# A recurrent two-tower scorer in fp32: the path's second layers as single products of 512 columns, and all engine orders rewritten with the path one step further ahead

## The reference, cut to what matters

```python
def _tower(x, w_in, b_in, blocks):
    h = _leaky(x @ w_in + b_in)
    for w1, b1, w2, b2 in blocks:          # two blocks, all 128 wide
        h = _leaky(_leaky(h @ w1 + b1) @ w2 + b2 + h)
    return h
...
def step(prev_delta, xk):
    fk, k = xk
    d = jnp.where(k == 0, fk[:, DELTA_IDX], jax.lax.stop_gradient(prev_delta))
    fk = fk.at[:, DELTA_IDX].set(d)
    fe = _tower(fk[:, :N_FLAT], fw_in, fb_in, flat_blocks)
    pe = _tower(fk[:, N_FLAT:], pw_in, pb_in, path_blocks)
    h = _leaky(jnp.concatenate([fe, pe], axis=-1) @ cw1 + cb1)
    delta = jax.nn.sigmoid(h @ cw2 + cb2)[:, 0]
    return (delta, delta)
```

## Time and profile before

| | |
|---|---|
| median of 3 runs | 1264.81 us (1264.74 to 1265.58) |
| the profiled execution's own time | 1264.49 us |
| its span in the trace | 1262.7 us |
| PE busy | 1243.4 us, 98% |
| PEld busy | 1062.1 us, 84% |
| ACT busy | 931.3 us, 74% |
| DVE busy | 888.8 us, 70% |
| POOL busy | 23.0 us, 2% |

### The profile page before, as it was taken

One profiled execution on the slowest core, in us unless ns is written; L12 is line 12 of the kernel. 1 busy time (PEld: TensorE's weight loads), 2 busy tenths in 40 slices (PEclk: granted clock), 3 DMA queues, 4 the chain that ended last, 5 costly groups with the idle time before them and its releaser, 6 DMA issues.

```text
span 1262.7 us, 20315 instructions
## 1 busy us (share of the span) xinstructions
PE 1243.4 (98%) x6022; PEld 1062.1 (84%) x6022; DVE 888.8 (70%) x1933; ACT 931.3 (74%) x2049; POOL 23.0 (2%) x20
## 2 busy tenths in 40 slices
PE   5999999999999999999999999999999999999998
PEld 3788888888888888888888888888888888888886
DVE  3677777777777777777777777777777777767775
ACT  2677777777777777777777777777777777777776
POOL 6000000000000000000000000000000000000000
PEclk9999999999999999999999999999999999999999
DMA  4400000000000000000000000000000000000000
GB/s 156 195 12 10 10 13 10 9 12 10 10 10 12 10 10 12 10 10 11 12 10 10 12 10 10 12 10 10 11 12 10 9 12 11 10 11 12 10 8 2
DMA packets 14177, 23.53 MB, mean 19 GB/s; under 512 B 6468, under 2 KB 6904, under 8 KB 13304
## 3 DMA queue, kind: packets, MB, share of 16 engines
q1 hardware_dynamic: 13640, 22.23, 6.0%
q10 hardware_dynamic: 432, 0.01, 0.0%
HBM read 15.66 MB, written 6.55 MB: 18 GB/s over the span
## 4 chain that ended last, share of the span: by engine, by line
PE 98%; DVE 1%; ACT 0%; issue 0%; DMA 0%; SPq 0%; DVEq 0%; ACTq 0%
PE ps_path L466 35%; PE ps_flat L466 18%; PE ps_res L469 18%; PE ps_head L567 9%; PE ps_head L562 9%; PE ps_path L484 2%; PE ps_head L580 2%; PE ps_head L575 2%; PE ps_flat L530 2%; DVE f_in L371 0%; DMA hidden_w<-hidden 0%; DVE p_sum L374 0%; PE ps_res L466 0%; DVE f_t L407 0%; SPq L201 0%
## 5 line engine op out<-in xcount | busy, mean ns | idle before, releaser
L257 ACT ACTIVATE f_mid<-ps_flat,columns_sb 128x256 f32<-128x256 f32 x512 | 242.7, 474 | 164.7 <-PE ps_flat L466 158.3
L466 PE MATMUL ps_path<-p_mid,hidden_w 128*128 128x256 f32 x1024 | 306.6, 382 | 0.8 <-ACT p_mid L257 0.8
L469 PE MATMUL ps_res<-f_mid,hidden_w 128*128 128x256 f32 x1024 | 305.6, 380 | 0.2
L257 ACT ACTIVATE f_res<-ps_res 128x256 f32<-128x256 f32 x512 | 196.4, 384 | 63.3 <-PE ps_res L469 63.3
L466 PEld LDWEIGHTS ps_path<-p_mid,hidden_w 128*128 128x128 f32 x1024 | 191.4, 191 | 33.2 <-ACT p_mid L257 2.4
L469 PEld LDWEIGHTS ps_res<-f_mid,hidden_w 128*128 128x128 f32 x1024 | 168.7, 189 | 54.1 <-ACT f_mid L257 1.7
L374 DVE SCALAR_TENSOR_TENSOR p_sum<-ps_path,columns_sb,p_in 128x512 f32<-128x512 f32 x128 | 96.1, 751 | 137.1 <-PE ps_path L466 137.1
L257 ACT ACTIVATE p_mid<-ps_path,columns_sb 128x512 f32<-128x512 f32 x256 | 176.2, 688 | 5.3 <-PE ps_path L466 5.3
L435 DVE CAST head_hi<-head 128x256 fp32r<-128x256 f32 x256 | 75.3, 294 | 136.2 <-ACT head L257 136.2
L407 DVE SCALAR_TENSOR_TENSOR f_t<-delta,columns_sb,ps_flat 128x256 f32<-128x256 f32 x256 | 123.2, 481 | 49.6 <-ACT delta L312 49.2
L466 PE MATMUL ps_flat<-f_in,hidden_w 128*128 128x256 f32 x512 | 153.2, 381 | 4.6 <-DVE f_in L371 4.5
(11 more groups left out here) (46 smaller groups left out, 1453.1 us busy)
## 6 DMA issues: line engine op xcount, KB each, us to landing
x_path<-x_hi SPq DMA_DIRECT2D x256, 16.0 KB
x_path<-x_lo SPq DMA_DIRECT2D x256, 16.0 KB
x_flat<-x_hi SPq DMA_DIRECT2D x256, 6.0 KB
x_flat<-x_lo SPq DMA_DIRECT2D x256, 6.0 KB
chunk_x<-x SPq DMA_DIRECT2D x2, 1152.0 KB, 7.2
x_hi<-chunk_hi SPq DMA_DIRECT2D x2, 1152.0 KB, 8.4
x_lo<-chunk_lo SPq DMA_DIRECT2D x2, 1152.0 KB, 10.1
out<-delta SPq DMA_DIRECT2D x128, 2.0 KB
```

The source lines that it names most:

```text
L257: return act.activation(dst, src, ACT.Prelu, bias=bias, alpha=NEG)
L466: return pe.matmul(dst, weight[w_name], src, start=True, stop=True)
L469: return pe.matmul(dst, weight[w_name], src, start=False, stop=True, skip_group_check=True)
```

## The change

LEAD becomes 4. `path_1b` and `path_2b` on PE lose their argument h and become one product of 512 columns each. The bodies of PE, ACT and DVE are written in a new order: the flat chain of group 1 now begins earlier (`flat_1a`, `flat_1b` and `flat_2a` of step k + 1 stand at the end of body k), `path_in` and `path_1a` work on step k + 4, `path_1b` on k + 4 (PE), `path_2a` and `path_2b` on k + 2. SP's and POOL's programs are unchanged. Lines 484 and below move up or down by a few: L530, L562, L567, L575 and L580 are L524, L556, L561, L569 and L574 after the change.

```diff
-LEAD = 3
+LEAD = 4
...
@@ ACT
             def body(k):
                 flat_1a(k, 0)
-                flat_1b(k, 1)
+                flat_2b(k, 1)
                 flat_1b(k, 0)
-                flat_2a(k, 1)
+                path_in(k + 4)
+                head_out(k, 1)
                 flat_2a(k, 0)
-                flat_2b(k, 1)
-                path_1b(k + 2)
+                path_2a(k + 2)
                 flat_2b(k, 0)
-                head_out(k, 1)
+                delta_out(k, 1)
                 head_out(k, 0)
-                path_in(k + 3)
-                delta_out(k, 1)
-                path_2a(k + 2)
+                path_1a(k + 4)
+                flat_1a(k + 1, 1)
                 delta_out(k, 0)
-                path_1a(k + 3)
-                flat_1a(k + 1, 1)
+                flat_1b(k + 1, 1)
+                path_1b(k + 3)
+                flat_2a(k + 1, 1)
...
@@ DVE
             def body(k):
                 flat_delta(k, 0)
                 flat_in(k, 0)
-                flat_1b_old(k, 1)
+                flat_2b_old(k, 1)
                 flat_1b_old(k, 0)
-                path_1b_sum(k + 2)
-                flat_2b_old(k, 1)
+                path_1b_sum(k + 3)
+                path_2b(k + 1)
                 flat_2b_old(k, 0)
-                path_2b_sum(k + 1)
-                path_2b(k + 1)
                 head_high(k, 1)
                 head_low(k, 1)
+                flat_delta(k + 1, 1)
+                flat_in(k + 1, 1)
                 head_high(k, 0)
                 head_low(k, 0)
-                flat_delta(k + 1, 1)
-                flat_in(k + 1, 1)
+                flat_1b_old(k + 1, 1)
+                path_2b_sum(k + 2)
...
@@ PE
-            def path_1b(k, h):
-                if exists(k):
-                    if h == 0:
-                        pe.wait_ge(s_p1a_h, k + 1)
-                        product(half(ps_path1, h), "pr1_w2", half(p_mid1, h))
-                    else:
-                        product(half(ps_path1, h), "pr1_w2", half(p_mid1, h)).then_inc(s_p1b_mm, 1)
+            def path_1b(k):
+                if exists(k):
+                    pe.wait_ge(s_p1a_h, k + 1)
+                    product(ps_path1[:, :], "pr1_w2", p_mid1[:, :]).then_inc(s_p1b_mm, 1)
...
```

More of the change, by code:

```diff
@@ L513, in path_2a, with path_2b @@
                         product(half(ps_path2, h), "pr2_w1", half(p_res1[par], h)).then_inc(s_p2a_mm, 1)
-            def path_2b(k, h):
+            def path_2b(k):
                 if exists(k):
-                    if h == 0:
-                        pe.wait_ge(s_p2a_h, k + 1)
-                        product(half(ps_path2, h), "pr2_w2", half(p_mid2, h))
-                    else:
-                        product(half(ps_path2, h), "pr2_w2", half(p_mid2, h)).then_inc(s_p2b_mm, 1)
+                    pe.wait_ge(s_p2a_h, k + 1)
+                    product(ps_path2[:, :], "pr2_w2", p_mid2[:, :]).then_inc(s_p2b_mm, 1)
             def flat_x(k, g):
@@ L584, in body @@
                 flat_1a(k, 0)
-                flat_1b(k, 1)
-                path_1b(k + 2, 1)
+                combine_path(k, 0)
+                flat_2b(k, 1)
                 flat_1b(k, 0)
-                flat_2a(k, 1)
-                path_2b(k + 1, 1)
+                flat_x(k + 1, 1)
+                path_in(k + 4)
+                combine_flat(k, 1)
                 flat_2a(k, 0)
-                flat_2b(k, 1)
-                combine_path(k, 0)
+                path_2a(k + 2, 0)
+                path_2a(k + 2, 1)
+                output_high(k, 1)
                 flat_2b(k, 0)
-                combine_flat(k, 1)
-                flat_x(k + 1, 0)
-                path_in(k + 3)
-                combine_flat(k, 0)
-                flat_x(k + 1, 1)
-                path_2a(k + 2, 0)
-                output_high(k, 1)
-                path_2a(k + 2, 1)
-                output_low(k, 1)
-                output_high(k, 0)
-                path_1a(k + 3, 0)
-                output_low(k, 0)
-                path_1a(k + 3, 1)
-                combine_path(k + 1, 1)
-                path_2b(k + 2, 0)
-                flat_1a(k + 1, 1)
-                path_1b(k + 3, 0)
+                output_low(k, 1)
+                path_1a(k + 4, 0)
+                path_1a(k + 4, 1)
+                combine_flat(k, 0)
+                path_2b(k + 2)
+                flat_1a(k + 1, 1)
+                output_high(k, 0)
+                combine_path(k + 1, 1)
+                output_low(k, 0)
+                flat_x(k + 1, 0)
+                flat_1b(k + 1, 1)
+                path_1b(k + 4)
+                flat_2a(k + 1, 1)
             pe.wait_ge(s_w_loaded, 16)
```

## The result

The changed kernel takes 1283.67 us (1283.22 to 1284.86, 4 runs) against 1264.78 (1264.64 to 1265.58): a ratio of 1.0147 [1.0135, 1.0159], or 18.9 us more. The forecast was 1276.5 with a range up to 1282.0. The direction was right; the loss was larger than the range allowed.

A forecast was written before the change was run, and what follows sets the result against it. PE was taken to bound the kernel, busy 98% at full clock with 9.58 us a step. The terms -1.2 + 4.6 + 2.3 + 4.6 + 1.7 gave +12.0 on 1264.5, so 1276.5 us, range 1269.5 to 1282.0.

The forecast's parts named there:

- Part 1: Merged path_1b and path_2b products on PE: two passes fewer each save 0.005 us a product, -1.2 us in all.
- Part 2: Group 1's second flat layer on PE: a wait of 0.036 us for ACT's f_mid in every step, +4.6 us.
- Part 3: The fill: path's chain and POOL's hold on DVE's p_res2 delay the first flat product, +2.3 us.
- Part 4: path_in of step 6: PE waits for loads queued behind chunk stores, +4.6 us, then half clock, +1.7 us.
- (c): Rival: a second thin cover also gives way, or the clock falls more often; 10 us more, 1286 us; chance 0.07.

The follow-up runs named there:

- x2_split: The changed kernel with path_1b and path_2b again as two products of 256 columns each, in the merged one's place: 1283.76 us, ratio 1.015.

## Why the prediction was wrong in size

**Part 1 (-1.2): nothing measurable.** The merged product's two passes start 0.429 us apart, 0.858 for a product where I had 0.863; the two products that x2_split has in its place take 0.863. So the 0.005 is there at the product, but the step shows 0.002 of the 0.010, and the runs show none.

**Part 2 (+4.6): the term that was mis-sized most.** With part 1 the forecast had 0.027 us a step; it is 0.061, over 127 steps 7.7 us in place of 3.4. ACT's part, 0.036, was right (0.033 with DVE's order mended). The sentence that failed is that no operation on DVE or ACT stands behind one that is ready later "except at the place named". flat_1b_old(k+1, 1) had all its inputs and stood behind head_low, which waits for ACT's head. I had looked at the durations of the new queue, and for the second layer at its wait for ACT alone, though its other input had moved to a new place. That is 0.028 a step, 3.5 us: DVE's add ends no later than f_mid, but its signal needs 0.12 us to the weight load and f_mid's 0.05. In the new place that is enough to bind PE.

**Long steps (no term): +1.5.** The kernel before has one, and it is the same thing: its head_low at 158.77 is DVE's number 319, 0.37 us late.

```profile
158.77 0.42 DVE L441 TENSOR_TENSOR head_lo<-head,head_hi 128x256 fp32r<-128x256 f32 x1 [0.48 <-DVE head_hi L435]
```

Its number 1983, at 851.09, is 0.32 late and lengthens no step. So the lateness was there before the change, and the covers took most of it. That DVE's places go by its own instructions is shown; what happens there is not, nor where TensorE's places lie and why two of them (36 and 39) moved with DVE's instructions. My rule for how far long steps move fell.

**Part 3 (+2.3): +2.46, the right number by luck.** The first flat product came at 35.87, some 0.2 late, and delta(0) 11.4 us after it as forecast. But the reason given, POOL's hold on p_res2, bound nothing: DVE's sum, which I had at about 31, was ready at 32.65, and PE, behind the path's chain, reached the flat product 0.25 us later than f_in allowed. Without the subtraction it came no sooner (36.18). So with POOL out of the way the term would not have been 0, as I wrote: the fill of the changed kernel stays as it is, 2.8 us behind the 44.79 of the kernel before, and 8.3 behind that kernel without the subtraction.

**Part 4 (+4.6 and +1.7): right in kind, 5.4 and 2.5 in size**, with the spread of the stores giving 8.1 back. 0.8 us of the wait is load_flat(3) ahead of store_delta(0) on SP: I counted from the delta's completion, and of the SP queue only what stands behind the store. The Trainium skill (TensorE: Matmul & The Clock Gate, "HAM oscillation — how this bites in real kernels") was right that a long DMA wait costs clock; the size, 4.9 us of PE's work at half, I had set at 3.4 us, from the stretch behind a shorter gap (4.2 us). In the kernel with split products the same wait left 3.41 us at half (66.20 to 69.62), so this term is not steadier than that.

In all: 4.3 (the step), 1.5 (long steps), 1.6 (step 6), 0.2 (fill), less 0.5 (mostly the kernel before's first two steps, which were 0.4 us longer), make the 7.1 us between the forecast's 12.0 and the 19.1 found. Of the rivals, (c) was nearest: a second cover did give way, by 0.03 and not 0.08 a step.

## What to carry to other kernels

When a queue is written anew, list for every product on the critical engine all its inputs and, for each, what stands ahead of its producer in that producer's queue: an order that is free on the busiest engine can still lose on the second one. Where a product waits for two signals, let the later one be the wait written first, which here was the load's own. A fill can hide the price of another change: settle first what binds it, in each kernel (the same eight pieces of a long GpSimd instruction gave the kernel before 5 us and the changed kernel nothing). Transfers that are issued in a burst behind an event of the run are late for whoever is moved forward; spread them.

## What the runs showed of the hardware

- Of two waits ahead of one product, the one written second is an event record of 0.05 us on PE. A signal that goes through it reaches the weight load 0.11 to 0.12 us behind its producer's end, the other 0.05. Swapped, this cost 0.034 and 0.032 us at two products of a step.
- DVE starts some of its instructions 0.31 to 0.37 us late. In the changed kernel and in the two with 40 instructions more all such starts in mid run are at record numbers 63 plus a multiple of 128 (319, 831, 1215, 1727 in the changed kernel), and an 8 KB transfer of the kind "instruction" starts within 0.73 us of each.
- A product of two columns from a 128 x 128 weight is no cheap filler: 40 of them delayed the first delta by 16.8 us at half clock, 0.42 each, and the weight loads, two to a product, are busy nearly all that time:

```profile
L466 PEld LDWEIGHTS ps_res<-hidden_w 128*128 128x128 f32 x84 | 18.2, 333 | 1.9 <-DVE cw_sign L367 1.7
```

- The clock rose in the fill at 29.3 to 32.1 us, differently for changed orders that do the same there, and the first delta moved with it by up to 1.3 us (47.23 to 48.51). Effects in the fill below that size were not told apart in single runs.
